# A four-layer transformer kernel: PSUM banks of three kinds of products, one weight step and one layer's output rows in later slots, and the order of the first loads

## The reference

```python
x = L0_attn_hidden_states                      # 4 sequences x 256 tokens x 512, fp32
for attention, ffn in layers:                  # written out four times
    xn = _layernorm(x, axis=-1)
    s = attention(xn)                          # 32 heads of 16
    g = _silu(ffn(xn))
    x = x + s * g
```

## Time and profile before

| | |
|---|---|
| runs | 1265.82, 1270.47, 1274.21 us |
| median | 1270.47 us |
| profiled execution | 1268.01 us |
| its span, first to last instruction | 1266.3 us |
| mean granted clock | 0.984 |

### The profile page before, as it was taken

How to read it: one execution, slowest core, us unless ns; L and a number is a source line. 1 busy time by engine, 2 the same in 40 slices (tenths; PEclk the granted TensorE clock), 3 DMA queues, 4 the chain that set the end, 5 groups by cost and what they waited for, 6 DMA issues and landing times.

```text
span 1266.3 us, 22363 instructions
## 1 busy us (share of the span) xinstructions
PE 1153.1 (91%) x8476; PEld 851.5 (67%) x8476; DVE 804.0 (63%) x1318; ACT 654.0 (52%) x1167; POOL 487.9 (39%) x692
## 2 busy tenths in 40 slices
PE   4899999999999999879999999999899888898897
PEld 3788877766656555545778787777667666675564
DVE  6753467776876665675644466536786878775444
ACT  3344358665554555554332433326865676666554
POOL 0000027454321111132545444414853565655453
PEclk9999989999999999999999999998999999999999
DMA  7000000030000000010232222201000001010001
GB/s 266 1 1 1 1 35 3 5 108 2 2 2 27 13 1 2 26 51 26 86 139 100 78 98 75 76 34 52 3 2 15 29 3 35 3 48 2 2 9 59
DMA packets 15260, 48.06 MB, mean 38 GB/s; under 512 B 2858, under 2 KB 6959, under 8 KB 14388
## 3 DMA queue, kind: packets, MB, share of 16 engines
q1 hardware_dynamic: 15156, 46.63, 10.6%
HBM read 44.00 MB, written 2.10 MB: 36 GB/s over the span
## 4 chain that ended last, share of the span: by engine, by line
PE 63%; DVE 21%; ACT 6%; issue 5%; DMA 2%; POOL 1%; SPq 0%; POOLq 0%; DVEq 0%; ACTq 0%
PE bank L667 17%; PE bank L783 12%; PE bank L697 8%; PE bank L911 8%; DVE negmax L1836 8%; PE bank L886 4%; PE bank L834 3%; PE bank L866 3%; ACT probs L1387 2%; DMA W_lo_whole<-in_w 2%; PE bank L800 1%; DVE W_lo_whole L1616 1%; DVE pvT L1862 1%; DVE rope_sin L1825 1%; DVE rope_cos L1821 1%
## 5 line engine op out<-in xcount | busy, mean ns | idle before, releaser
L1836 DVE TENSOR_REDUCE negmax<-bank 128x4 f32<-128x1024 f32 (+1 forms) x256 | 250.1, 1016 | 87.8 <-PE bank L843 68.2
L1387 ACT ACTIVATE probs<-bank 128x1024 f32<-128x1024 f32 (+1 forms) x256 | 218.5, 867 | 62.0 <-PE bank L866 59.4
L2061 POOL TENSOR_SCALAR_AFFINE_SELECT probs<-probs 128x512 f32<-128x512 f32 x192 | 124.1, 656 | 199.9 <-ACT probs L1387 199.7
L1982 POOL TENSOR_TENSOR W_lo<-W_lo_whole,W_hi 128x512 fp32r<-128x512 f32 x84 | 117.0, 1422 | 103.1 <-ACT W_hi L1129 103.1
L2030 POOL TENSOR_TENSOR scaled<-pvT,recip 128x128 f32<-128x128 f32 x128 | 57.8, 451 | 234.7 <-DVE recip L1864 231.2
L834 PE MATMUL bank<-kT,qT 64*128 64x256 f32 (+1 forms) x1024 | 104.6, 298 | 23.0 <-DVE negmaxT L1854 7.5
L886 PE MATMUL bank<-probs,V 128*32 128x256 f32 (+1 forms) x2048 | 116.7, 345 | 7.1 <-DVE negmax L1836 2.7
L866 PE MATMUL bank<-qT,kT 64*128 64x256 f32 (+1 forms) x640 | 112.4, 381 | 9.2 <-ACT qT L1367 3.8
L1397 ACT ACTIVATE pv<-bank 128x256 f32<-128x256 f32 x128 | 49.4, 386 | 125.4 <-PE bank L886 124.6
L1129 ACT ACTIVATE W_hi<-W_lo_whole 128x1536 fp32r<-128x1536 f32 x28 | 41.7, 1488 | 134.1 <-DVE W_lo_whole L1616 134.1
L834 PEld LDWEIGHTS bank<-kT,qT 64*128 64x128 f32 x1024 | 80.0, 188 | 37.8 <-issue 13.3
(11 more groups left out here) (206 smaller groups left out, 2639.8 us busy)
## 6 DMA issues: line engine op xcount, KB each, us to landing
W_lo_whole<-in_w SPq DMA_DIRECT2D x28, 768.0 KB, 4.1
Wqkv_lo_whole<-in_Wqkv SPq DMA_DIRECT2D x6, 768.0 KB, 6.9
Wo_lo_whole<-in_Wo SPq DMA_DIRECT2D x4, 1024.0 KB, 4.9
Wqkv<-in_Wqkv SPq DMA_DIRECT2D x2, 1536.0 KB, 7.0
Wdown_whole<-in_Wd SPq DMA_DIRECT2D x1, 2816.0 KB, 15.6
x<-in_x SPq DMA_DIRECT2D x4, 512.0 KB, 6.0
out<-x SPq DMA_DIRECT2D x8, 256.0 KB, 2.0
V_lo_whole<-in_V SPq DMA_DIRECT2D x1, 1408.0 KB, 6.0
```

The lines of the kernel that those rows point to most:

```text
L1387: nc.scalar.activation(A[l].probs[gi % 2][kb][:, :, q0 - kb * A[l].probs1:].rearrange("p (b h) q -> p b h q", b=2), B.tensor(key)[:, :, 0: ...
L1836: v.tensor_reduce(A[l].negmax[u % 2][:, qb, :].rearrange("p (b h) -> p b h", b=2)[:, :, 2 * g:2 * g + 2], B.tensor(key)[:, :, 0:2 * nk].re ...
L1982: ins = gp.tensor_tensor(lo, whole, hi.bitcast(F32), ALU.subtract)
L2061: gp.affine_select(out=blk, in_=blk, compare_op=ALU.is_ge, fill=0.0, base=0, pattern=[[0, 4], [1, P]], channel_multiplier=-1).then_inc(cau ...
```

## The change

It has six parts, and computes the same products in the same three-term form. (1) The turned maxima of layer 1 go to bank 2 instead of 0. (2) Output products at group 0 of the odd units go to bank 2 instead of 1; those at group 2 stay in bank 1. (3) The int4 products all go to bank 2. (4) Scaling, rounding and low part of layer 2's weight chunk 1 move from slot (14, 2) to (14, 3). (5) In run 1, layer 3's third set of output rows moves from slot (14, 3), both tiles (banks 4 and 5), to (15, 0) and (15, 2), one tile each, both in bank 4; run 0 keeps (14, 3). (6) The loads of x's sequences 2 and 3 are issued behind Wg, Wu and the signs.

```diff
-MAX_BANK = {True: 5, False: 0}
+MAX_BANK = {True: 5, False: 2}
...
-WEIGHTS2_SLOTS = {(13, 2): 0, (14, 2): 1, (15, 1): 2}
+WEIGHTS2_SLOTS = {(13, 2): 0, (14, 3): 1, (15, 1): 2}
...
     n = sequence(r, U // 2 - 1)
-    if U == RUN - 2:
+    if r == 0 and U == RUN - 2:
         return [n + (0,), n + (1,)] if g == 3 else []
+    if r == 1 and U == RUN - 1:
+        return [n + (g // 2,)] if g % 2 == 0 else []
     return [n + (g // 2,)] if U % 2 == 1 and 1 < U < RUN - 1 and g % 2 == 0 else []
...
                 for n in rows_projected(r, U, g):
-                    project_out(*n, 1 if U % 2 == 1 else (4, 5)[n[2]])
+                    project_out(*n, (2 if g == 0 and U < RUN - 1 else 1) if U % 2 == 1 and U < RUN - 1 else 4 if r == 1 else (4, 5)[n[2]])
...
                 if r == 0 and (U, g) in TILE1_SLOTS:
-                    tile1(TILE1_SLOTS[U, g], (U, g) == (12, 3))
+                    tile1(TILE1_SLOTS[U, g], 2)
...
             load(ident[:], a["ident"], ident_in)
-            for b in range(SEQS):
+            for b in range(2):
                 load(x[:, 2 * b:2 * b + 2, :], xv[:, 2 * b:2 * b + 2, :], x_in[b])
             load(compact0[0][:], a["Wg0"], ffn_in[0])
             load(compact0[1][:], a["Wu0"], ffn_in[1])
             load(sign_in[:], a["sign_in"], signs_in)
             load(sign_hid[:], a["sign_hid"], signs_in)
+            for b in range(2, SEQS):
+                load(x[:, 2 * b:2 * b + 2, :], xv[:, 2 * b:2 * b + 2, :], x_in[b])
             load(W0_whole[2][:], a["Wd0"], ffn_in[2])
```

## The result

| | before | with the change |
|---|---|---|
| median of the runs | 1271.14 us (1265.82 to 1274.21, 4 runs) | 1251.07 us (1244.98 to 1252.94, 4 runs) |
| profiled execution, its span | 1268.01, 1266.3 us | 1252.94, 1251.2 us |

The ratio is 0.9857, 95% interval 0.9821 to 0.9892: 1.4% faster, 18 us by the ratio (14 to 23). Forecast were 1256 us and a gain of 14.7; between the two profiles the span shrank by 15.1. (A ratio here is worked out from all the runs together, and need not equal the quotient of the two medians beside it.)

What follows compares the result with a forecast made beforehand. TensorE, busy 1153.1 of 1266.3 us, was taken to bound the kernel. Terms -2.4 -3.1 -3.8 -1.3 +1.1 -5.2 = -14.7 from 1268.0 gave 1253.3, plus 2.5 to the median: 1256 us, range 1249 to 1267.

Steps and rivals of the forecast that it cites:

- A: Program start: with two loads of x issued behind it, Wu lands earlier and absum starts sooner; -2.4 us, at most 3.28.
- B: Output products at group 0 of odd units: bank 2 ends their waits for DVE's row maxima; -3.1 us, clock uncounted.
- C: Layer 2's first FFN product: moving the weights' low part shortens the 3.12 us wait and ends low clock; -3.8 us.
- D: Layer 1's turned maxima in bank 2: row-score waits shrink by 0.34 us each, four of the larger paying; -1.3 us.
- E: Int4 products in bank 2: two gate waits shrink (-0.7), two new waits in slots (11, 0), (13, 0) (+1.8); +1.1 us.
- F: Layer 3's third output rows leave slot (14, 3): (15, 0) starts 10.96 us earlier, later slots absorb the products; -5.2 us.
- that banks give nothing: Rival: bank moves hand their 0.70 and 0.34 us to the next wait for DVE; 1261 us, chance 0.18.
- That the clock falls all the same: Rival: clock still falls behind the shortened waits at layer 2's first product and layer 3's third rows; 1259 us, chance 0.13.
- The loads did land earlier: Answers the rival that the change of loads does nothing, Wu landing when it did; 1258 us, chance 0.07.
- Bank 2 as the queue: Rival: 28 groups newly hold bank 2 ahead of column scores, each paying 0.88 us; slower, 1284 us, chance 0.06.
- New waits for bank 2: Sign of being wrong: TensorE's new waits for bank 2 sum to more than 5 us.
- New stretches of low clock: Sign of being wrong: new stretches of low granted clock turn up, each costing some 1.6 us.

Runs made afterwards that it cites:

- the two timings: Two timed comparisons of the whole changed kernel with the kernel before: ratio 0.9857 at first, 0.9873 when run again unedited beside the follow-up kernels.
- B alone: Kernel before with only the output products of group 0 of odd units moved to bank 2: 1261.32 against 1267.86 us, ratio 0.9940.
- the rows part alone: Kernel before with only layer 3's third output rows moved to slots (15, 0) and (15, 2): 1262.67 against 1267.86 us, ratio 0.9964.

## Why the prediction was right, and where not

The bound, the places, the direction and the side on which the time lies were right, and the time falls in the range. By steps, with what the matched starts show:

| step | forecast | measured |
|---|---|---|
| A, loads | -2.4 | -1.7 on average at the first product (-1.2 at 50 us), -2.9 between the two profiles |
| B, output products | -3.1 | -4.0 of waits, -2.7 of clock |
| C, low part | -3.8 | -3.45 |
| D, maxima | -1.3 | -0.9 |
| E, int4 products | +1.1 | +1.5 |
| F, third rows | -5.2 | -5.0 |
| sum | -14.7 | -16 |

B's clock is 15/8 less 1/5 of a stretch, 1.7, times 1.6 us. E is the 2.1 of the two slots less 0.6 that the gates gave. The measured sum stands beside 18.2 (13.7 to 22.8) and 16.1 (12.4 to 19.8) from the two timings. It leaves out all clock that is not explained (in the two profiles 489, 1150 and the end, 7.8 us against the change), so the agreement bears out the size of the whole and not each term.

**The step that failed is B's sentence that nothing is counted for the clock**, "but the two other waits of 0.70 have no such fall behind them". That argued from one execution that the wait does not decide, and it left out the fourth wait, the 0.75 marked as issue: behind it the clock fell in that same execution (0.55 from 1095.50, shown above), so two of four waits had a fall. Eight traces without the part have nearly two such stretches each, the one at slot (11, 0) in every trace; five traces with it have one in all. Removing the waits removes most of these falls, and that is worth their mean number. The bound of 1.7 for one fall was too small for the same reason. Together with the waits (4.0 by matched starts, where 3.1 was forecast: each product starts 0.1 to 0.2 us earlier than its wait alone accounts for) B was the largest part and not the third.

For A, 2.4 lies close to absum's 2.6, in part by luck: Wu landed 3.0 us earlier, more than was worked out, and DVE was not free to use it all. What came next was missed: tscale now waits 0.90 us for PE's sums, behind the transposes. Of the wait of absum in the profile before, which had the latest landing of Wu of seven, 0.8 us was not the order's. As to the HBM figure cited from the Trainium skill ("DMA: Bandwidth & Descriptors", "Where 436 GB/s comes from"), its estimate of 2.9 us is nearer to the 3.0 by which Wu's landing moved than the 2.4 of the row's 438 GB/s. With landings that scatter by 1.4 us in one order the traces do not settle the rate.

C's wait went from 3.12 to 0.92, where 0.8 was forecast, and the clock with it. D moved as forecast, with four steps, each smaller than the 0.34 worked out: 7.5 us of waits became 3.6 and 2.7, and the gain was the matmuls that run first. F's next late thing was named and stood there, 0.94 us where 0.7 was worked out.

E was right in sign and mechanism, and low in size: two waits of 0.78, but 2.1 us by the matched starts once they are taken out. The rule of the Trainium skill cited there ("Perfetto Trace Analysis", "Matmuls") holds in this trace at those two slots. Elsewhere bank 2 is taken by 26 other groups, with no new wait at B's and with those of D and of the gates merely moved, since a bank that has been emptied by the time it is claimed costs nothing, however often it is used.

The rivals: that banks give nothing fell with B alone (7.6 us). That the clock falls all the same was seen once, in the rows part alone. The loads did land earlier. Bank 2 as the queue did not come: only E's two waits of 0.78 at that price, not 28.

The prediction's own signs of being wrong both turned up, and did not mean what it took them for. New waits for bank 2 sum to 6.3 us, over its 5, but 4.7 of them are waits of bank 0 that moved, and only E's 1.6 are added. New stretches of low clock stand at 489, 1148 and the end, and the gain came in spite of them. A sign that does not tell moved waits from added ones, or a stretch gained from one lost elsewhere, says little about the time.

What stays open: the low clock of the last 18 us, 4.7 us of PE's lead, that near 1150, 1.4 us, and that at 489, 1.7 us. Every trace with the whole change has the first two and neither trace of the kernel before has them at that length, but some kernels with one part have them and some not. Whether the change brings them on or they depend on something else is not settled.

## What to carry to other kernels

When a bank conflict is taken away, look at what next claims the new bank: if its holder is emptied before that claim, the wait goes whole (output products); if not, it only moves and pays the few instructions in between (maxima, gates). Two groups that follow each other at once should not share one: here each such pair cost 1.0 to 1.1 us. And a short stall ahead of a run of large products can cost more than itself, since the clock may fall behind it (1.6 us a fall here): read several profiles before calling such a fall accidental.

## What the runs showed of the hardware

A wait of 0.70 to 0.75 us ahead of 12 products of 128x512 was followed by a stretch of 1.2 GHz 15 times of 32 (four such waits a trace, in eight traces): eight times of eight at one place, never at another, seven times of sixteen at the two others. Without the wait it was one of twenty. The same code in the same place ran at full clock in one execution and at half in the next (slot (5, 0) in the two profiles of the kernel before: a granted clock of 0.55 from 959.00, and 1.00 from 952.00). In one order of issue, the landing of a 680 KB load varied by 1.4 us between executions (absum from 12.65 to 14.06), and one of a 768 KB load by 1.8 us (issued at 648.36 and 646.58, scaling at 654.39 and 650.77).
